# A convolution stage's two ends: statistics gathered in two sets, first image and taps prepared in the stage before

## The reference, cut to what matters

```python
out = relu(batchnorm(conv(x, ternarize(w1)), g1, b1))                 # 1x1, 96 -> 576 channels
out = relu(batchnorm(conv(out, ternarize(w2), pad=1, groups=576), g2, b2))  # 3x3 depthwise
out = batchnorm(conv(out, ternarize(w3)), g3, b3)                     # 1x1, 576 -> 96
x = out + x
# batchnorm: mean and var over axes (0, 2, 3), so over all 32 images
```

## Time and profile before

| | us |
|---|---|
| median of 3 runs | 5873.81 |
| lowest and highest | 5856.16 and 5875.26 |
| the profiled execution | 5871.17 |
| its span | 5869.3 |

### The profile page before, as it was taken

How to read it: one execution, slowest core, us unless ns; L and a number is a source line. 1 busy time by engine, 2 the same in 40 slices (tenths; PEclk the granted TensorE clock), 3 DMA queues, 4 the chain that set the end, 5 groups by cost and what they waited for, 6 DMA issues and landing times. The chain is left out here.

```text
span 5869.3 us, 145952 instructions
## 1 busy us (share of the span) xinstructions
PE 5416.5 (92%) x59604; PEld 3550.5 (60%) x59604; DVE 3610.0 (62%) x6670; ACT 3419.5 (58%) x5674; POOL 1704.1 (29%) x964
## 2 busy tenths in 40 slices
PE   4979999999999799999679999999999999999996
PEld 4956666666666444444257667667667667666663
DVE  1036666666666723333327777777777777777775
ACT  2445555555555366676446666666666666666652
POOL 0037777777777400000011111111111111111110
PEclk9989999999999899999869888999988999989986
DMA  3646766666666499999745655665665665665551
GB/s 84 157 117 159 174 164 170 170 170 168 167 173 159 117 326 326 333 340 334 235 142 145 165 162 153 167 163 154 165 163 153 166 170 157 164 168 155 161 136 44
DMA packets 553171, 1041.24 MB, mean 177 GB/s; under 512 B 178512, under 2 KB 347280, under 8 KB 535888
## 3 DMA queue, kind: packets, MB, share of 16 engines
q1 hardware_dynamic: 552512, 1031.93, 63.7%
HBM read 552.39 MB, written 478.94 MB: 176 GB/s over the span
## 5 line engine op out<-in xcount | busy, mean ns | idle before, releaser
L718 POOL TENSOR_TENSOR hlo<-h,hhi 128x1682 f16<-128x1682 f32 x288 | 977.2, 3393 | 447.8 <-DVE hhi L749 447.8
L733 DVE BATCH_NORM_STATS2 stats<-z 128x6 f32<-128x392 f32 x1152 | 597.3, 560 | 517.6 <-ACT z L670 507.7
L1514 POOL TENSOR_TENSOR y<-zin,x_tok 96x448 f32<-96x448 f32 x224 | 263.2, 1176 | 2199.5 <-ACT zin L1470 2198.0
L680 ACT ACTIVATE h<-c1ps,s 128x1512 f32<-128x1512 f32 x288 | 465.1, 1615 | 696.7 <-PE c1ps L596 696.7
L888 PE MATMUL pps<-z2m,w3T 128*96 128x392 f32 x2048 | 709.7, 499 | 19.0 <-ACT z2m L865 18.9
L617 PE MATMUL dwps<-hhi,taps 64*64 64x392 f16 x13824 | 689.0, 330 | 2.5 <-issue 2.4
L617 PE MATMUL dwps<-hlo,taps 64*64 64x392 f16 x13824 | 681.4, 327 | 1.4 <-issue 1.3
L865 ACT ACTIVATE z2m<-z2m,s 128x784 f32<-128x784 f32 x512 | 490.9, 1029 | 262.3 <-DMA z2m<-z_scratch 262.2
L1522 POOL TENSOR_TENSOR onat<-tb,o 96x448 f32<-96x448 f32 x224 | 238.6, 1065 | 1150.8 <-DVE o L1581 1150.8
L888 PEld LDWEIGHTS pps<-z2m,w3T 128*96 128x96 f32 x2048 | 322.8, 163 | 396.5 <-issue 343.1
L617 PEld LDWEIGHTS dwps<-hlo,taps 64*64 64x64 f16 x13824 | 406.1, 106 | 179.3 <-issue 2.8
(11 more groups left out here) (218 smaller groups left out, 10038.4 us busy)
## 6 DMA issues: line engine op xcount, KB each, us to landing
z_scratch<-z SPq DMA_DIRECT2D x1152, 196.0 KB, 3.3
z2m<-z_scratch SPq DMA_DIRECT2D x128, 1568.0 KB, 20.1
a_scratch<-a SPq DMA_DIRECT2D x224, 384.0 KB, 2.8
bt<-a_scratch SPq DMA_DIRECT2D x96, 672.0 KB, 8.8
c_scratch<-cc SPq DMA_DIRECT2D x128, 336.0 KB, 4.7
d<-c_scratch SPq DMA_DIRECT2D x128, 336.0 KB, 4.7
xa<-in_x_dram SPq DMA_DIRECT2D x32, 1176.0 KB, 7.3
xin<-in_x_dram SPq DMA_DIRECT2D x32, 1176.0 KB, 8.7
```

The lines of the kernel that those rows point to most:

```text
L680: nc.scalar.activation(to, src, ACT.Relu, bias=s1[:, 1, u:u + 1], scale=s1[:, 0, u:u + 1]).then_inc(h_ready, 1)
L718: nc.gpsimd.tensor_tensor(to, h, hi, ALU.subtract).then_inc(lo_ready, 1)
L733: nc.vector.bn_stats(stats[:, i, v, at:at + 6], z2[:, v % 3, g, r, :]).then_inc(s_stat, 1)
```

## The change

The tensors `xin`, `xhi`, `xlo`, `t1h`, `h32`, `wv` and `taps`, their semaphores and the helpers `xhi_scalar` and `xlo_pool` move out of conv into a scope that is open in gram and conv. In gram, SP issues the loads of images 0 and 1 behind its last `xa` load; ACT splits image 0 behind its last `xT` copy, ahead of its wait for the square root; POOL, which had no work in gram, subtracts behind it; DVE clears `h32`, casts `t1h` and makes `taps` ahead of its first addition to `gacc`.

The statistics of conv are aggregated in two sets: pairs 0 to 12 (`gather_early`, one at a time, spread over units of pairs 13 and 14) and pairs 13 to 15 (`gather_late`: two in each of the last 6 units of the last pair, six behind the last unit). The two are added with the weight 13 to 3, in one more DVE operation; the factor behind PE's sum is changed to fit.

```diff
@@ gram
+                for m in range(2):
+                    sp.dma_start(xin[:, m, :], x[m]).then_inc(ldx[m], 16)
...
+                for c in range(NCH):
+                    xhi_scalar(act, 0, 0, c)
                 act.wait_ge(s_var, 1)
                 nc.scalar.activation(gtmp[0][:, :], gtmp[0][:, :], ACT.Sqrt).then_inc(s_std, 1)
+
+            @block.gpsimd
+            def _(pool):
+                for c in range(NCH):
+                    xlo_pool(pool, 0, 0, c)
...
                 nc.vector.memset(xT[:, :, :, C:C + 1], 1.0).then_inc(s_init, 1)
...
+                nc.vector.memset(h32[:, :, :, :], 0.0).then_inc(s_zero, 1)
+                nc.vector.tensor_copy(t1h[:, :], t1e[:, 0:PL]).then_inc(s_taps, 1)
+                w = w2t[:, :, :].rearrange("p u (y x) -> p u y x", y=3)
+                even, odd = lane[:, 32:33], lane[:, 33:34]
+                tap_link(nc.vector.tensor_scalar(wv[:, 0, 0, :, :], w[:, :, 0, :], even, None, ALU.mult))
...
+                for da in range(2):
+                    for y in range(2):
+                        to = taps[:, :, da, :, y, :]
+                        v = wv[:, da, y, :, :].unsqueeze(3).broadcast_to([128, UN, 3, 32])
+                        nc.vector.tensor_tensor(to, one.rearrange("p (u x) c -> p u x c", u=UN), v,
+                                                ALU.mult).then_inc(s_taps, 1)
                 dve.wait_ge(xt_used, NG)
@@ conv
             @block.sync
             def _(sp):
-                for m in range(2):
-                    sp.dma_start(xin[:, m, :], x[m]).then_inc(ldx[m], 16)
                 conv_sync(sp, 0, False, True)
...
             @block.scalar
             def _(act):
                 act.wait_ge(s_zero, 1)
-                for c in range(NCH):
-                    xhi_scalar(act, 0, 0, c)
                 conv_scalar(act, 0, False, True)
...
             @block.gpsimd
             def _(pool):
-                for c in range(NCH):
-                    xlo_pool(pool, 0, 0, c)
                 conv_pool(pool, 0, True)
...
+            LAST = 3
+            EARLY = NP - LAST
+            gathered = [(u, g) for u in range(UN) for g in range(2)]
+
+            def gather_early(dve, u, g):
+                dve.wait_ge(s_stat, EARLY * NV * 4)
+                nc.vector.bn_aggr(mvs[:, 0, u, g, :], stats[:, 0:EARLY, u:u + UN + 1:UN, 12 * g:12 * g + 12]
+                                  ).then_inc(s_aggr, 1)
+
+            def gather_late(dve, u, g):
+                dve.wait_ge(s_stat, (NN - UN + u + 1) * 4)
+                nc.vector.bn_aggr(mvs[:, 1, u, g, :], stats[:, EARLY:NP, u:u + UN + 1:UN, 12 * g:12 * g + 12]
+                                  ).then_inc(s_aggr, 1)
+
+            def gather(dve, i, v):
+                n = (i - EARLY) * NV + v - 4
+                if 0 <= n < 2 * NV - 8:
+                    for u, g in gathered[n * NV // (2 * NV - 8):(n + 1) * NV // (2 * NV - 8)]:
+                        gather_early(dve, u, g)
+                u = v - UN - 3
+                if i == NP - 1 and u >= 0:
+                    for g in range(2):
+                        gather_late(dve, u, g)
 
             def conv_vector(dve, i, before):
                 for v in range(NV):
...
                     if late is not None:
                         copy_second(dve, *late)
                         take_stats(dve, *late, 1)
+                    gather(dve, i, v)
...
-                dve.wait_ge(s_stat, NN * 4)
-                for u in range(UN):
+                for u in range(NV - UN - 3, UN):
                     for g in range(2):
-                        link(nc.vector.bn_aggr(mv[:, u, g, :], stats[:, :, u:u + UN + 1:UN, 12 * g:12 * g + 12]))
-                sq = wv[:, :, :, :, :].rearrange("p a b u x -> p (a b u x)")[:, 0:2 * UN]
-                m, e = (mv[:, :, :, k].rearrange("p u g -> p (u g)") for k in range(2))
+                        gather_late(dve, u, g)
+                dve.wait_ge(s_aggr, 4 * UN)
+                sq = wv[:, :, :, :, :].rearrange("p a b u x -> p (a b u x)")[:, 0:4 * UN]
+                m, e = (mvs[:, :, :, :, k].rearrange("p s u g -> p (s u g)") for k in range(2))
                 link(nc.vector.tensor_tensor(sq, m, m, ALU.mult))
-                nc.vector.tensor_tensor(e, e, sq, ALU.add).then_inc(s_mix, 1)
+                link(nc.vector.tensor_tensor(e, e, sq, ALU.add))
+                old, new, both = (q.rearrange("p u g k -> p (u g k)") for q in (mvs[:, 0], mvs[:, 1], mv[:, :, :, :]))
+                nc.vector.scalar_tensor_tensor(out=both, in0=old, scalar=EARLY / LAST, in1=new, op0=ALU.mult,
+                                               op1=ALU.add).then_inc(s_mix, 1)
                 dve.wait_ge(s_mixed, 1)
```

More of the change, by code:

```diff
@@ L365, in _, with xhi_scalar, xlo_pool @@
                     link(nc.vector.tensor_scalar(diag[:, :, 4 + k:5 + k], diag[:, :, 1 - k:2 - k], -1.0, None, ALU.mult))
+        pre = keep.enter_context(ExitStack())
+        xin = sb("xin", [C, 2, TOK], ctx=pre)
+        xhi = sb("xhi", [C, 2, W, W], F16, ctx=pre)
+        xlo = sb("xlo", [C, 2, W, W], F16, ctx=pre)
+        t1h = sb("t1h", [C, PL], F16, ctx=pre)
+        h32 = sb("h32", [128, 3, SL, PW], ctx=pre)
+        wv = sb("wv", [128, 2, 2, UN, 3], ctx=pre)
+        taps = sb("taps", [128, UN, 2, 3, 2, 32], F16, ctx=pre)
+        ldx = [sem(f"conv_x_loaded{m}", pre) for m in range(2)]
+        xhi_ready = sem("xhi_written", pre)
+        xlo_ready = sem("xlo_written", pre)
+        s_zero = sem("borders_zero", pre)
+        s_taps = sem("taps_ready", pre)
+        s_wv = sem("tap_chain", pre)
+        def xhi_scalar(act, j, m, c):
+            if c == 0:
+                act.wait_ge(ldx[m], j * 16 + 16)
+            to = xhi[:, m, ROWS * c:ROWS * c + ROWS, :].rearrange("p a b -> p (a b)")
+            nc.scalar.activation(to, xin[:, m, c * CH:c * CH + CH], ACT.Copy).then_inc(xhi_ready, 1)
+        def xlo_pool(pool, j, m, c):
+            pool.wait_ge(xhi_ready, (2 * j + m) * NCH + c + 1)
+            rows = slice(ROWS * c, ROWS * c + ROWS)
+            to, hi = (q[:, m, rows, :].rearrange("p a b -> p (a b)") for q in (xlo, xhi))
+            nc.gpsimd.tensor_tensor(to, xin[:, m, c * CH:c * CH + CH], hi, ALU.subtract).then_inc(xlo_ready, 1)
         st = ExitStack()
@@ L506, in build @@
         with st:
[L507 to L511, removed]
             hhi = sb("hhi", [128, 3, SL, PW], F16, ctx=st)
@@ L514, in build @@
             z2 = sb("z2", [128, 3, 2, 2, QN], ctx=st)
-            wv = sb("wv", [128, 2, 2, UN, 3], ctx=st)
-            taps = sb("taps", [128, UN, 2, 3, 2, 32], F16, ctx=st)
             stats = sb("stats", [128, NP, 2 * UN, 24], ctx=st)
+            mvs = sb("mvs", [128, 2, UN, 2, 2], ctx=st)
             mv = sb("mv", [128, UN, 2, 2], ctx=st)
@@ L522, in build @@
             dw = st.enter_context(nc.psum_tensor("dwps", [128, 2, 2, 512], F32))
[L523 to L527, removed]
             c1_full = sem("conv1_done", st)
@@ L538, in build @@
             s_ch = sem("conv_chain", st)
+            s_aggr = sem("z2_stats_gathered", st)
             s_mix = sem("mix_in", st)
@@ L651, in split_of @@
                 return (i, 1, v - 1) if 1 <= v <= NCH else (i + 1, 0, v - 10) if more and 10 <= v < 10 + NCH else None
[L653 to L663, removed]
             def copy_first(act, i, v):
@@ L761, in link @@
                     dve.wait_ge(s_ch, chain[0])
[L763 to L777, removed]
-                        to = taps[:, :, da, :, y, :]
-                        v = wv[:, da, y, :, :].unsqueeze(3).broadcast_to([128, UN, 3, 32])
-                        nc.vector.tensor_tensor(to, one.rearrange("p (u x) c -> p u x c", u=UN), v,
-                                                ALU.mult).then_inc(s_taps, 1)
                 conv_vector(dve, 0, False)
@@ L804, in _ @@
                           s2[:, 1, :], (gtmp[0][:, :], gtmp[1][:, :]), s_var, s_std, 0)
+        pre.close()
         st = ExitStack()
```

15 lines of the change are left out of this document (14 added, 1 removed).

## The result

| | before | changed |
|---|---|---|
| median, us (4 runs each) | 5865.6 | 5808.36 |
| lowest and highest | 5856.16 and 5875.26 | 5802.32 and 5813.98 |
| profiled execution | 5871.17 | 5809.97 |
| its span | 5869.3 | 5807.3 |

The changed kernel takes 0.9902 of the time of before (95% interval 0.9879 to 0.9926): 57 us less, between 43 and 71. The forecast was 5825, in a range of 5804 to 5836. A fourth run of before moved its median from 5873.81 to 5865.6.

A forecast was written before the change was run, and what follows sets the result against it. PE bounds the depthwise stage, but it idles at conv's start and end; gains of 16.8 and 31.3 us sum to 48.1, taking the 5871.17 us profiled execution to 5823.1. Forecast 5825 us, range 5804 to 5836.

The forecast's parts named there:

- Part 1: Start of conv: first image, taps and cleared buffers moved into gram let PE start at 352.5, not 369.27; gain 16.8 us.
- SP's row: Barrier before conv: SP began 0.50 us behind DVE's last gram instruction, the early bound for PE's start.
- the forecast's own list: Signs of a wrong prediction: gram ends later, pairs 13 and 14 exceed 5.65 us a unit, or SP's store wait ends conv.
- Rival (a): Start of conv: PE slow out of the barrier, at 354.4 or later, part 1 gains 14.9 or less; 5828 us, chance 0.10.
- Rival (b): End of gram: last xa load held up by the two behind it, PE waits 6 us; 5831 us, chance 0.05.
- Part 2: End of conv: aggregations in two sets cut 35.1 us behind the last statistics to 3.8; gain 31.3 us.
- Rival (c): End of conv: an aggregation costs 1.89 us whatever its size, gaining 22.9 instead of 31.3; 5834 us, chance 0.04.
- In the loop, cost 0: Conv pairs 13 to 15: early and late aggregations fit beside PE at cost 0, upper bound 29 us.
- Rival (d): Conv pairs 13 to 15: gathers partly reach PE, 4 to 29 us; 5829 to 5854 us, chance 0.07.
- The first slack: Conv unit: DVE idles 1.72 of 5.65 us, so a 1.6 us gather fits with 0.1 us to spare.
- the second one: Conv unit: another 1.7 us between DVE's copy of the second half and PE's overwriting of its bank.
- Rival (e): Conv pairs 13 and 14: gathers starve PE, clock halves, a unit takes 11.3 us; slower, 5895 us, chance 0.01.

The follow-up runs named there:

- part 1 alone: Changed kernel with conv's end as before (one set of aggregations), against the kernel before: 5848.01 us against 5863.35, ratio 0.9977.
- the repeat: The changed kernel timed again without an edit, against the kernel before: 5816.86 us, ratio 0.9917.
- part 2 alone: Kernel before with the statistics aggregated in two sets, first image still split in conv: 5836.89 us against 5863.35, ratio 0.9944.
- two aggregations: Changed kernel with each early aggregation made twice, the second into an unread scratch tensor; ran once, 5801.26 us.
- 5.9 us a gather: Changed kernel with each early aggregation made four times, copies into an unread scratch tensor: ratio 0.9999 of the kernel before.

## Why the prediction was right, point by point

- **Part 1, 16.8 us forecast.** The first matmul came 15.9 us earlier in the first profile, 16.7 with part 1 alone, 17.7 in the repeat. Two terms were off and nearly cancel. PE's start behind the barrier: I took DVE's 1.61 us, and it was 0.68. In the changed kernel the moved memset again shows 1.00 us of "issue" ahead of it, inside a stage and behind no barrier; so most of the 1.62 us in the earlier trace rows belonged to that instruction and not to the barrier. SP's row, 0.50, was the better one. And gram's chain grew by 0.71 us beside POOL, which I had put into the range as 1 us and not into the sum. By the forecast's own list a gram that ends later was a sign of being wrong; in the first profile it ended 1.8 us later, of which the change explains these 0.7.
- **Rival (a), PE slow out of the barrier, fell**: its first matmul came 0.68 us behind DVE's last instruction and 0.18 us behind SP's first issue. The Trainium skill ("Runtime: NRT & Kernel Launch", section "Instruction fetch mechanics") says that a branch taken to a page that has not been fetched makes an engine wait for the fetch. The trace shows no room for such a wait here, and no run shows whether the branch was of that kind.
- **DVE, ACT, POOL and SP in gram**: covered, as forecast. Taps ended at 89.4 (forecast 90), xhi at 339.5 (338.9), xlo at 344.2 (345.3). Rival (b) fell: PE shows no wait for a load but the very first; the two behind the last one did not hold it up.
- **Part 2, 31.3 us forecast.** The aggregations and hand-over shrank from 35.06 to 2.9 us (2002.30 to PE's 2005.2), 32.2 us, just over the 32 that had been given as the most. The early one was 1.547 us (forecast 1.56). The late one was 0.424 us (forecast 0.48), and six took 2.15, not 3.1: they are not chained, and start about 0.35 us apart, less than one lasts. I had added a pitch where this edit takes it away. The Trainium skill ("VectorE: DVE Perf Modes", section "The TRN2 errata") gives a fixed term that is 0.156 us at 0.96 GHz, as an estimate; the line through the two new sizes leaves 0.424 - 72 x 4.68 ns = 0.087 us, so for these short unchained ones the measurement is below it. Rival (c), 1.89 us whatever the size, fell. The stores were in 2.3 us ahead of the chain's end, where 3 had been worked out; they would be the next to end last.
- **In the loop, cost 0**: part 2 alone spent 1646.7 us there and before 1647.7. Rival (d) fell. The first slack, DVE's gap, was enough. Of the second one only a part shows: with two aggregations a gather is 1.3 us longer than the gap, and PE's longest wait for the copy is 0.8 us. That it is 1.7 us, as forecast, no run shows.
- **Rival (e), slower**: at 5.9 us a gather the gain is eaten up, and conv's end comes 10 us later than before, but the time is not measurably longer. Its term of 5.65 us a unit for the clock was far too large: the half level was granted for some 31 us over 18 such units.
- **The sum**: 48.1 forecast, 47.4 between the marks, 46.3 from the parts, 48.6 from both in five rounds. The first comparison's 57 us lie above it, its interval of 43 to 71 holds it. The forecast of 5825 was 17 us above the measured median. Of these 8 come from its start at 5873.81, a median of three that lay 8 us above that of four, and 9 from the difference between 57 and 48, which the five rounds did not repeat. The range, down to 5804, held the result by 4 us, and only because it went down by the whole spread of before: that is room for noise, and in part luck, and no term of the mechanism.

## What to carry to other kernels

Where all engines meet at the end of a stage, look at what each side of the meeting waits for in a row: work that needs nothing of the stage before (first loads, splits, tables, cleared buffers) fits into engines that are idle there, and a statistic over everything can be gathered over nearly everything beforehand. Ask each time what ends last once the chain is short; here those two steps were worth 33 us at conv's end, and 2.6 of 5.3 us at project's, where the stores came next. Judge a change of 1% in a kernel with a spread of 1% by the marks in two traces, by its parts alone and by several rounds, not by one pair of profiles: one stage that nobody touched moved by 19 us between executions.

## What the runs showed of the hardware that I had not expected

- A DVE copy of 96x576 f32 beside POOL's tensor_tensor took 1.17 us instead of 0.46, while the first of two such copies, also beside POOL, kept its 0.46. POOL's operation took 1.31 us on average when DVE's taps lay beside part of the row (9.18 for seven), 1.06 beside gram's chain (7.41) and 1.00 with DVE idle (6.97). The taps themselves took 5.64 us beside it and 3.96 without.
- bn_aggr on DVE is close to a line from 72 to 1536 values: 0.424, 1.547, 1.889, 6.634 and 7.085 us for 72, 312, 384, 1440 and 1536. Without a semaphore chain six of 72 values start about 0.35 us apart.
- Whether an unchanged kernel spends 2978 or 2998 us in tokens is decided anew in each execution. The length goes with the time that the clock is granted at the half level; what decides that was not tried.
